# Reordering the MLP stage between attention and convolution on one NeuronCore: GELU and ReLU blocks, table loads and PSUM banks

## What is computed

```python
# layer 0: a transformer block over the channels of every pixel
xc = xc + window_attention(layernorm(xc))                 # windows of 8x8 pixels, 8 heads
h  = gelu(layernorm(xc) @ w_mlp1 + b_mlp1, approximate=False) @ w_mlp2 + b_mlp2
x  = xc + h
# layer 1: a gated, dynamic convolution
h      = einsum('bchw,oc->bohw', x, pw1_w) + pw1_b
scores = sigmoid(relu(mean(h) @ fc1 + b) @ fc2 + b)       # mean over the pixels
mask   = top 32 channels of scores, per image
h      = relu(h);  offsets = tanh(mean(h) @ off_w + off_b)
w_k    = dw_k * (1 + sigmoid(offsets[k, 0])) + tanh(offsets[k, 1])       # k = 3x3, 5x5, 7x7
out    = pw(concat_k(depthwise(h * mask, w_k))) + pw_b + x
```

## Time and profile before

| what | value |
|---|---|
| median of 3 runs | 324.87 us (323.93 to 325.02) |
| the profiled execution, its own time | 324.21 us |
| its span in the trace | 322.4 us |
| mean granted TensorE clock over the span | 0.974 of full speed |
| TensorE busy | 289.2 us, 90% of the span |
| VectorE busy | 235.0 us, 73% |
| ScalarE busy | 203.0 us, 63% |
| GpSimd busy | 107.3 us, 33% |

### The profile page before, as it was taken

One profiled execution on the slowest core, in us unless ns is written; L12 is line 12 of the kernel. 1 busy time (PEld: TensorE's weight loads), 2 busy tenths in 40 slices (PEclk: granted clock), 3 DMA queues, 4 the chain that ended last, 5 costly groups with the idle time before them and its releaser, 6 DMA issues.

```text
span 322.4 us, 6206 instructions
## 1 busy us (share of the span) xinstructions
PE 289.2 (90%) x2314; PEld 211.3 (66%) x2314; DVE 235.0 (73%) x456; ACT 203.0 (63%) x343; POOL 107.3 (33%) x144
## 2 busy tenths in 40 slices
PE   2648979999999999999989797898999999999993
PEld 2236766878878686886868543453577777777772
DVE  4867437589798888979787336679999999976211
ACT  6696633948667685865535788987953746754400
POOL 4151425756576567555441601231310000000000
PEclk9986989999999999999979999999999999999998
DMA  6870383434244333424430000590008659767811
GB/s 162 178 156 31 84 188 85 104 76 90 71 98 89 78 84 76 103 67 96 101 71 2 0 2 0 115 212 14 2 0 169 130 113 196 141 137 147 182 33 33
DMA packets 17276, 29.94 MB, mean 93 GB/s; under 512 B 5536, under 2 KB 12192, under 8 KB 17248
## 3 DMA queue, kind: packets, MB, share of 16 engines
q1 hardware_dynamic: 13792, 22.72, 30.9%
q0 software_dynamic: 2880, 6.03, 11.0%
q10 hardware_dynamic: 576, 0.81, 1.0%
HBM read 4.22 MB, written 2.10 MB: 20 GB/s over the span
## 4 chain that ended last, share of the span: by engine, by line
PE 76%; DVE 7%; ACT 5%; SPq 4%; DMA 4%; issue 2%; POOL 0%; DVEq 0%; ACTq 0%
PE psum L1089 27%; PE psum L868 13%; PE psum L791 5%; PE psum L865 5%; PE psum L884 5%; PE psum L1013 3%; PE psum L844 3%; DVE maxima L1209 3%; SPq L379 3%; PE psum L1001 3%; PE psum L813 3%; DMA k_heads<-k_parts 3%; PE psum L892 2%; PE psum L818 2%; PE psum L823 2%
## 5 line engine op out<-in xcount | busy, mean ns | idle before, releaser
L1089 PE MATMUL psum<-shifted,conv_w 128*128 128x512 f32 x336 | 86.5, 419 | 0.0
L1089 PEld LDWEIGHTS psum<-shifted,conv_w 128*128 128x128 f32 x336 | 63.9, 191 | 21.6 <-issue 1.3
L868 PEld LDWEIGHTS psum<-q_heads,k_blocks 128*128 128x128 f32 x384 | 56.1, 194 | 6.5 <-issue 3.0
L868 PE MATMUL psum<-q_heads,k_blocks 128*128 128x256 f32 x384 | 57.3, 286 | 0.0
L1209 DVE TENSOR_REDUCE maxima<-psum 128x8 f32<-128x512 f32 x64 | 40.1, 683 | 12.2 <-PE psum L844 12.0
L603 ACT ACTIVATE probs<-psum 128x512 f32<-128x512 f32 x64 | 37.5, 603 | 18.2 <-PE psum L868 18.0
L461 POOL DMA_DIRECT2D k_blocks<-k_parts x56 | 32.2, 583 | 11.5 <-PE psum L868 11.5
L865 PE MATMUL psum<-minus_max,pick 128*128 128x512 f32 x64 | 32.7, 511 | 0.5 <-ACT probs L603 0.3
L844 PE MATMUL psum<-k_heads,q_blocks 128*128 128x256 f32 x128 | 24.0, 314 | 9.5 <-DMA k_heads<-k_parts 6.9
L791 PE MATMUL psum<-parts,center_average 128*128 128x512 f32 x64 | 22.6, 436 | 8.7 <-DVE parts L287 7.1
L287 POOL TENSOR_TENSOR parts<-x,parts 128x256 fp32r<-128x256 f32 (+1 forms) x21 | 19.4, 938 | 32.0 <-ACT parts L552 22.2
(11 more groups left out here) (142 smaller groups left out, 468.1 us busy)
## 6 DMA issues: line engine op xcount, KB each, us to landing
shifted<-images SPq DMA_DIRECT2D x32, 332.5 KB, 5.5
q_heads<-q_parts SPq DMA_DIRECT2D x128, 32.0 KB, 2.2
k_blocks<-k_parts POOLq DMA_DIRECT2D x56, 64.0 KB
k_heads<-k_parts SPq DMA_DIRECT2D x64, 32.0 KB, 2.3
out<-x SPq DMA_DIRECT2D x8, 256.0 KB, 4.8
q_blocks<-q_parts POOLq DMA_DIRECT2D x28, 64.0 KB, 2.5
x<-in_x SPq DMA_DIRECT2D x6, 256.0 KB, 6.2
x<-in_x SPq DMA_DIRECT2D x4, 128.0 KB, 4.0
```

What stands on the lines that cost most here:

```text
L868: ins = pe.matmul(bank[:, hh * G // 2:(hh + 1) * G // 2], k_blocks[:, hh, w // (NW // 2), k_part, w % (NW // 2), :], of_half(q_heads[:, q_ ...
L1089: ins = pe.matmul(psum[:, CONV0 + bh, :], conv_w[bh][:, w_part, t, :], img[:, y:y + H - 1:2, x0:x0 + W], start=t == 0 and w_part + part == ...
```

## The change

Four things are changed together. ScalarE does `gelu(3)` and `relu(1)` ahead of the two table loads and the last layer norm's statistics instead of behind them. The pointwise products of groups 0 and 1 share bank 7, so that group 1 no longer has to wait until the last variance has been read from bank 2; it waits instead until `relu(0)` and `pool_image(0)` have read bank 7. `mlp2(7)` writes bank 5 (one of the banks of `mlp1`) and therefore waits for the last GELU instead of for `add_mlp(6)`. The lists of TensorE and VectorE are reordered around that, and GpSimd clears a row of the second image's weights one entry later, behind another semaphore.

```diff
+        def pointwise_bank(n):
+            return PW1[0] if n == 0 or n % 2 else PW1[1]
+
+        def mlp_bank(n):
+            return MLP if n < NG - 1 else HIDDEN0 + 2
...
@@ GpSimd
                 low_image(n, n // 2, n % 2)
-                if n == 2:
-                    pool.wait_ge(S["pe_mlp1"], 4 * (NG // 2))
+                if n == 3:
+                    pool.wait_ge(S["dv_normed2"], 2 * NG)
                     no_row(1)
@@ ScalarE
             relu(0, 0, 0)
+            gelu(3, 1)
+            relu(1, 0, 1)
             load_tables(LN_AND_EXP)
             inverse_deviation2(NG - 1)
             load_tables(GELU)
-            relu(1, 0, 1)
-            gelu(3, 1)
             gelu(4, 0)
@@ TensorE, mlp2 and pointwise1
-                if n > 0:
+                if n == NG - 1:
+                    pe.wait_ge(S["ac_gelu"], 4 * NG)
+                elif n > 0:
                     pe.wait_ge(S["dv_x2"], n)
...
                 if n == 1:
+                    pe.wait_ge(S["ac_relu"], 1)
+                    pe.wait_ge(S["dv_hsum"], 1)
+                if n == 2:
                     pe.wait_ge(S["ac_log2"], NG)
-                if n > 1:
+                if n > 2:
                     pe.wait_ge(S["ac_relu"], n - 1)
                     pe.wait_ge(S["dv_hsum"], n - 1)
@@ TensorE, its list
             mlp1(4)
+            mlp2(3, 1)
+            pointwise1(2, 0)
             gate_means(0)
-            pointwise1(2, 0)
+            mlp1(5, range(0, 2))
             gate_scores(0)
-            mlp2(3, 1)
-            mlp1(5, range(0, 2))
-            gate_spread(0)
             mlp1(5, range(2, 4))
             pointwise1(3, 1)
+            gate_spread(0)
             mlp2(4, 0)
...
             pointwise1(5, 1)
+            mlp2(6, 0)
             gate_means(1)
-            mlp2(6, 0)
+            mlp2(7, 1)
             pointwise1(6, 0)
             gate_scores(1)
-            mlp2(7, 1)
@@ VectorE, its list
             pool_image(0, 0, 0)
+            add_mlp(2)
+            pool_image(1, 0, 1)
             normalise2(NG - 1)
+            gate_means(0)
+            add_mlp(3)
+            gate_hidden(0)
             high_of_normed2(NG - 1)
+            gate_scores(0)
+            gate_spread(0)
             for bh in range(2):
                 low_of_normed2(NG - 1, bh)
-            pool_image(1, 0, 1)
-            gate_means(0)
-            add_mlp(2)
-            gate_hidden(0)
-            gate_scores(0)
-            gate_spread(0)
-            add_mlp(3)
             pool_image(2, 1, 0)
+            add_mlp(4)
             gate_mask(0)
             gate_taps(0)
-            add_mlp(4)
+            products(0, 0)
             pool_image(3, 1, 1)
-            products(0, 0)
+            add_mlp(5)
             add_products(0, 0)
-            add_mlp(5)
+            gate_means(1)
             pool_image(4, 2, 0)
-            gate_means(1)
+            add_mlp(6)
             products(0, 1)
-            add_mlp(6)
             gate_hidden(1)
             low_even(0, 0)
             add_products(0, 1)
             pool_image(5, 2, 1)
+            add_mlp(7)
             gate_scores(1)
             gate_spread(1)
-            add_mlp(7)
```

More of the change, by code:

```diff
@@ L714, in relu @@
                 act.wait_ge(S["po_images"], n + NBORDER - 1)
-                bank = psum[:, PW1[half], :]
+                bank = psum[:, pointwise_bank(n), :]
                 act.activation(relu_out[:, half, :], bank, ACT.Relu, bias=vec[:, 9:10], accum_out=r_sum[:, n:n + 1])
@@ L1012, in mlp2 @@
                             pe.wait_ge(S["ac_gelu"], 4 * n + 2 * bh + 2)
-                        ins = pe.matmul(psum[bh * C:(bh + 1) * C, MLP, :], mlp2_w[:, f, :], hidden[:, par, 2 * bh + f, :],
+                        ins = pe.matmul(psum[bh * C:(bh + 1) * C, mlp_bank(n), :], mlp2_w[:, f, :], hidden[:, par, 2 * bh + f, :],
                                         start=f == 0, stop=f == 1)
@@ L1020, in pointwise1 @@
                 if n == 1:
+                    pe.wait_ge(S["ac_relu"], 1)
+                    pe.wait_ge(S["dv_hsum"], 1)
+                if n == 2:
                     pe.wait_ge(S["ac_log2"], NG)
-                if n > 1:
+                if n > 2:
                     pe.wait_ge(S["ac_relu"], n - 1)
                     pe.wait_ge(S["dv_hsum"], n - 1)
-                pe.matmul(psum[:, PW1[half], :], pw1_w, x2[:, bass.ds(n * G, G)], start=True, stop=True).then_inc(S["pe_pw1"], 1)
+                pe.matmul(psum[:, pointwise_bank(n), :], pw1_w, x2[:, bass.ds(n * G, G)], start=True, stop=True).then_inc(S["pe_pw1"], 1)
             def gate_means(k):
@@ L1256, in add_mlp @@
                 mine = x2[:, bass.ds(n * G, G)]
-                dve.scalar_tensor_tensor(mine, psum[:, MLP, :], vec[:, 8:9], mine, ALU.add, ALU.add).then_inc(S["dv_x2"], 1)
+                dve.scalar_tensor_tensor(mine, psum[:, mlp_bank(n), :], vec[:, 8:9], mine, ALU.add, ALU.add).then_inc(S["dv_x2"], 1)
             def high_of_normed2(c):
@@ L1333, in pool_image @@
                 dve.wait_ge(S["ac_relu"], n + 1)
-                dve.tensor_reduce(h_sum[:, bass.ds(n, 1)], psum[:, PW1[half], :], AX.X, ALU.add).then_inc(S["dv_hsum"], 1)
+                dve.tensor_reduce(h_sum[:, bass.ds(n, 1)], psum[:, pointwise_bank(n), :], AX.X, ALU.add).then_inc(S["dv_hsum"], 1)
             def step_done(k, n):
```

## The result

The changed kernel is slower: 325.52 us median of 9 runs (324.12 to 328.14), against 324.07 us for the kernel before in the same set (9 runs, 322.35 to 325.02). The ratio is 1.0067, 95% interval 1.0039 to 1.0094. The direction and the place were forecast; the size was forecast as 1.2 us, 0.37%, and the ratio says about twice that, 2.2 us; by the medians it is 1.45.

What follows compares the result with a forecast made beforehand. TensorE, 90% busy, was taken as the bound, the first weights only 0.6 us behind. Weights at 220.0 plus 1.9 of stalls, then 8.08 of copies, start the convolution 1.2 us later: 326.1 us, range 323.9 to 327.0.

Steps and rivals of the forecast that it cites:

- TensorE's lead: TensorE in the MLP stage: pointwise1(1) 1.4 us sooner, mlp2(4) starting at 209.8 and ending about 2.5 us sooner.
- The mask behind `add_mlp(4)`: On VectorE, add_mlp(4) waits for mlp2(4), so the first gate's mask begins at 212.4, 2.0 us later than before.
- The two collisions: GpSimd's subtractions of groups 3 and 4 hold VectorE in mask and taps, then products: 0.9 and 1.0 us.
- one stall: Rival, chance 0.24: only one GpSimd subtraction holds VectorE; convolution starts at 229.2, +0.3 us, 325.2.
- of none: Rival, chance 0.12: neither GpSimd subtraction holds VectorE; convolution starts at 228.3, -0.6 us, 324.3.
- The weights: First image's weights summed on VectorE at 221.9 to 222.0; ScalarE's copies take 8.08 us, to 230.1.
- TensorE's lead coming through: Rival, chance 0.08: the mask does not really wait, TensorE bounds; convolution starts by 227.5, -1.4 us, 323.5.
- off every path: GpSimd's moved clearing of a row was said to lie on no path that sets the time.
- The start of the convolution: TensorE starts within 0.1 us of the last weight copy, at about 230.15 instead of 228.94: +1.2 us.
- The time: Whole execution: 325.4 us against the profiled 324.21, and 326.1 from the runs' median of 324.87.

Runs made afterwards that it cites:

- busy waits: Changed kernel with two idle products on TensorE in each of its two waits of 2.2 us; 325.19 us, ratio 1.0039 to the kernel before.
- second profile: The changed kernel run once more, unedited; 326.08 us, ratio 1.0065 to the kernel before.
- no collision: Changed kernel with GpSimd's low_image(3) held until the first image's weights are summed; 324.05 us, ratio 1.0025 to the kernel before.
- mask first: Changed kernel with add_mlp(4) put back behind gate_mask(0) and gate_taps(0) on VectorE; 323.63 and, again, 322.27 us, ratios 0.9997 and 0.9934 to the kernel before.

## Why the prediction was right, and where it was short

- TensorE's lead: right. `mlp2(4)` was to start at 209.8 and started at 208.99 with a stage that began 0.73 us sooner: +15.3 both ways. The gap ahead of `pointwise1(1)` is 0.41 us, 0.1 above what I gave.
- The mask behind `add_mlp(4)`: right. It was to begin at 212.4, which is +17.97; it began at +17.94. VectorE's wait ahead of the addition was 0.95 us, not 1.2. (In the kernel before, TensorE was not yet at `mlp2(4)` when the mask began at 210.36; it came to it at 212.24. The sum does not rest on that sentence.)
- The two collisions: right. Charged 0.9 and 1.0 us; measured 1.24 - 0.29 = 0.95 and 1.83 - 0.82 = 1.01, and both gone when GpSimd was held. The rivals of one stall and of none fall with it: in each of the two profiles of the changed kernel both are there. One row was read too freely: the pooling at 214.96 shares only 0.05 us with the subtraction at 213.80, so it does not show that a pooling is left alone; the pooling at 196.89, 0.69 us long and wholly beside a subtraction that runs from 196.94 to 198.13, does. Here the rule of the Trainium skill (SBUF — State Buffer, section Who interferes with whom), that a VectorE instruction with two SBUF inputs is excluded by a GpSimd instruction that reads SBUF, went further than the rows of before did, which had it for large sums only; the mask step of 128 columns was held as well, 1.23 and 1.24 us.
- The weights: right. Last copy forecast at 230.1, +35.7; measured +35.69 and +35.67. The second image's weights did not become late.
- TensorE's lead coming through: refuted; it waits 2.2 us twice, at the two places named.
- GpSimd's cleared row "off every path": nearly. It runs from 213.58 to 214.41 beside VectorE's small steps, and some 0.09 us of the delay lie there.
- The start of the convolution: this is the step that was short. "TensorE starts within 0.1 us" holds where the clock is up at that point (0.10 with busy waits and in the second profile), but in the first profile TensorE came 0.84 us after the weights, since most of `mlp2(7)` ran at half the clock. My sum let `mlp2(7)`, `pointwise1(6)` and the gate product end at 229.5, 0.6 us to spare, from durations at full clock; I named the two new gaps and did not ask what they do to the clock. The term is 0.76 us in the profile in which it bites; the stage then loses 2.02 instead of 1.2, and the ratio of 1.0067, 2.2 us, has that size. In the second profile the term is 0.0 there, the stage loses 1.26 us as forecast, and 0.42 us appear ahead of `gate_spread(1)`.
- The time: 326.1 was forecast from a median of 324.87 and 325.52 measured; the span, 323.7, is only 0.1 above the sum. That both are so close is luck. For the span, the missing 0.8 us of the clock and the 0.7 us by which that execution reached the stage sooner nearly cancel. For the time, the median I started from, 324.87, lay 0.8 us above the 324.07 of the nine runs that the change was measured against; from 324.07 the same sum gives 325.3.

The change does what it says: the early GELU and the shared bank bring TensorE 2.5 us ahead. The gain went into a new wait. An addition that TensorE needs was put ahead of a mask that ScalarE and the convolution need; that delayed the mask by 2.0 us and led it and the products into two collisions, and the gaps that opened on TensorE brought its clock down.

## What to carry to other kernels

When an engine that is nearly always busy gains time, ask which other chain ends at the same point: here the weights were ready only 0.6 us before TensorE came to them, and their chain set the new start. For each entry of an engine's list, ask which chain waits for it and how much that chain has to spare: one addition moved behind the mask in VectorE's list was worth 2.7 to 3.5 us. A wait of TensorE had a second price here, since its clock fell: two waits of 2.2 us that the sum held to be covered cost up to 0.76 us. Count such waits before calling them hidden. And read an edit to one stage from marks inside that stage, since here the medians of one kernel moved by up to 1.4 us between sets.

## What the runs showed of the hardware that was not expected

- The same program at the same place got half the clock in different spots: from 225.1 us, inside the second of two gaps of 2.2 us, in one execution, and from 221.0, at the end of the first, in the other, each time for 3.4 us. With the gaps filled by idle products it stayed at 1.00. Without the collisions it did so from 222.8 us, with a single gap of that length. In the kernel with ScalarE's order and the bank alone, it was at half for 6.8 us, from inside the wait of 5.13 us on.
- What GpSimd's subtraction held was not large instructions only: a step of 128x128 took 1.24 us instead of 0.29. VectorE lost nearly what was left of the subtraction when its instruction's turn came, whatever the instruction's size: with 1.15, 1.09, 0.72 and 0.35 us left it lost 1.01 and 0.95 (changed kernel), 0.59 (no collision, line 1444) and 0.22 (mask first, line 1442).
- A VectorE instruction with a single SBUF input was held too, which the reading of the rows in the prediction did not have: the gate's TENSOR_SCALAR of 2x64 at line 1393 took 1.17 us instead of 0.18 beside the subtraction at 231.59 us of the changed kernel.
- Executions of kernels that are equal up to the MLP stage reached it between 193.09 and 195.86 us. In the one that came last the granted clock was 0.97 between 60 and 120 us of the span and 1.00 there in all the other profiles; what the rest of the spread is was not looked into. Inside the stage, marks of the two profiles of the changed kernel agreed within 0.02 us up to the last weight copy.
